# Experts' second layer with both weight halves in one 512-column product, and row transposes placed inside the first layer

## The reference, cut to what matters

```python
onehot = one_hot(argmax(softmax(t @ Wr)), 8)         # 4096 tokens, 8 experts
disp   = zeros(8 * 640, 256).at[flat].add(t * kept)  # 640 rows for each expert
h      = relu(einsum('ecd,edf->ecf', disp.reshape(8, 640, 256), W1))   # W1 256 x 1024
eout   = einsum('ecf,efd->ecd', h, W2)                                 # W2 1024 x 256
out    = where(kept, eout[flat] * pmax, t)
x      = layernorm(x + out)
```

## Time and profile before

| what | value |
|---|---|
| median of 3 runs | 936.65 us (935.19 to 936.7) |
| profiled execution, its own time | 935.7 us |
| span of its core | 933.9 us |
| mean granted TensorE clock | 0.937 |
| PE busy over the span | 791.7 us (85%) |
| experts' part of the span | 658 to 934 us |

### The profile page before, as it was taken

How to read it: one execution, slowest core, us unless ns; L and a number is a source line. 1 busy time by engine, 2 the same in 40 slices (tenths; PEclk the granted TensorE clock), 3 DMA queues, 4 the chain that set the end, 5 groups by cost and what they waited for, 6 DMA issues and landing times. The chain is left out here.

```text
span 933.9 us, 16891 instructions
## 1 busy us (share of the span) xinstructions
PE 791.7 (85%) x5933; PEld 632.4 (68%) x5933; DVE 581.5 (62%) x1410; ACT 402.1 (43%) x639; POOL 356.0 (38%) x290
## 2 busy tenths in 40 slices
PE   5999883589999999999999897872799999999992
PEld 3777662456666766666676664541699999999982
DVE  4888855465777777777777876532345554654542
ACT  4666540235545655555555555530433323422320
POOL 0333334433355545544545452232225134424422
PEclk9999887889999999999999999865799999999997
DMA  3115701554445434544554334003422243234000
GB/s 126 46 28 156 208 1 51 153 152 124 127 143 165 151 113 134 153 139 135 160 154 137 119 119 126 23 31 111 147 91 86 86 129 119 63 111 139 21 28 19
DMA packets 75913, 100.91 MB, mean 108 GB/s; under 512 B 10961, under 2 KB 63354, under 8 KB 75856
## 3 DMA queue, kind: packets, MB, share of 16 engines
q1 hardware_dynamic: 72400, 92.03, 33.1%
q0 software_dynamic: 3456, 8.13, 2.5%
HBM read 65.47 MB, written 35.74 MB: 108 GB/s over the span
## 5 line engine op out<-in xcount | busy, mean ns | idle before, releaser
L984 DVE TENSOR_REDUCE nmax<-ps_m 128x4 f32<-128x1024 f32 x128 | 156.6, 1223 | 52.5 <-PE ps_m L744 40.5
L938 ACT ACTIVATE pt<-ps_a 128x1024 f32<-128x1024 f32 x128 | 131.4, 1026 | 99.4 <-PE ps_a L754 75.8
L1249 ACT ACTIVATE hid<-ps_h 128x640 fp32r<-128x640 f32 x64 | 45.1, 705 | 151.0 <-PE ps_h L1189 151.0
L1189 PE MATMUL ps_h<-xt,w_hi 128*128 128x320 f32 x512 | 99.9, 317 | 1.0 <-DVE xt L1264 1.0
L1298 DVE SCALAR_TENSOR_TENSOR hid<-ps_h,hid 128x640 fp32r<-128x640 f32 x64 | 52.8, 824 | 56.0 <-ACT hid L1249 55.5
L744 PE MATMUL ps_m<-kst,qst 48*128 48x256 f32 x512 | 65.6, 334 | 25.6 <-DVE nmax L984 23.0
L1201 PE MATMUL ps_y<-w_hi,hid 128*128 128x256 f32 x640 | 85.3, 284 | 1.7 <-issue 1.7
L1189 PEld LDWEIGHTS ps_h<-xt,w_hi 128*128 128x128 f32 x512 | 79.9, 191 | 5.5 <-DVE hid L1298 3.0
L1201 PEld LDWEIGHTS ps_y<-w_hi,hid 128*128 128x128 f32 x640 | 80.1, 191 | 1.9 <-issue 1.9
L744 PEld LDWEIGHTS ps_m<-kst,qst 48*128 48x128 f32 x512 | 39.1, 188 | 61.3 <-DVE nmax L984 32.3
L621 POOL TENSOR_TENSOR half<-kq,half 128x512 fp32r<-128x512 f32 x32 | 41.6, 1301 | 96.6 <-ACT half L876 91.7
(11 more groups left out here) (169 smaller groups left out, 1586.9 us busy)
## 6 DMA issues: line engine op xcount, KB each, us to landing
halves_dram<-half SPq DMA_DIRECT2D x64, 256.0 KB, 2.5
gated<-in_w SPq DMA_DIRECT2D x16, 1024.0 KB, 5.4
kst<-halves_dram SPq DMA_DIRECT2D x64, 128.0 KB, 2.6
qst<-halves_dram SPq DMA_DIRECT2D x64, 128.0 KB, 3.0
rows_dram<-blank SPq DMA_DIRECT2D x1, 5160.0 KB, 19.6
gated<-rows_dram SPq DMA_DIRECT2D x8, 645.0 KB, 4.2
x_raw<-in_x_t SPq DMA_DIRECT2D x8, 512.0 KB, 3.9
xres<-in_x SPq DMA_DIRECT2D x16, 256.0 KB, 3.4
```

Source lines behind the costliest of these rows:

```text
L938: nc.scalar.activation(pt[:, k % 4].rearrange("p s t q -> p (s t q)"), ps_a[:].rearrange("p s t q -> p (s t q)"), ACT.Exp).then_inc(s["exp ...
L984: nc.vector.tensor_reduce(nmax[:, q, :, :, h // 2].rearrange("p t s -> p s t"), ps_m[:], AX.X, ALU.max, negate=True).then_inc(s["max_done" ...
L1189: mm = pe.matmul(ps_h[:, f % 2, c2, 0:HC], w1[a][:, p, k, f * P:(f + 1) * P], xt[:, b, p, k, c2 * HC:(c2 + 1) * HC], start=(n == 0 and k = ...
L1249: nc.scalar.activation(hid[:, HI, f, :].rearrange("p (c n) -> p c n", c=2), ps_h[:, f % 2, :, 0:HC], ACT.Relu).then_inc(s["hid_hi"], 1)
```

## The change

The two split halves of W2 become one tile in which, for each block f, the 256 high columns and the 256 low columns lie side by side. For each row tile `down` multiplies `hid` HI by all 512 columns (8 products; `hi*hi` into the first half of the bank, `hi*lo` into the second), then `hid` LO by the 256 high columns, added to the first half. For tile 0 the HI products wait block by block for `hid_hi`, and only the LO products wait for all of `hid_lo`. DVE adds the second half of the bank (times gate, plus row) into `res` first, raises `res_part`, waits for it, and adds the first half. The three turns of the next expert's rows now follow hidden blocks 4, 5 and 6 on PE, ACT and DVE alike; SP and POOL keep their order.

```diff
--- before.py
+++ after.py
@@ -1106,7 +1106,7 @@
     new = gated[:, 1, 0:2 * TS * D].rearrange("p (b t d) -> p b t d", b=2, t=TS)
     rows = gated[:, 3, 0:2 * TS * ROW].rearrange("p (b t r) -> p b t r", b=2, t=TS)
     w1 = [T("w1_hi", [P, 2, KD, F], F32R), T("w1_lo", [P, 2, KD, F], F32R)]
-    w2 = [T("w2_hi", [P, 2, FT, D], F32R), T("w2_lo", [P, 2, FT, D], F32R)]
+    w2 = T("w2", [P, 2, FT, 2, D], F32R)
     xt = T("xt3", [P, 2, 2, KD, CAP], F32R)
     hid = T("hid", [P, 2, FT, CAP], F32R)
     st, mv, ve = T("st4", [P, TS, 6], F32), T("mv4", [P, TS, 2], F32), T("ve4", [P, TS], F32)
@@ -1117,12 +1117,13 @@
     ps_h = PS("ps_h", [P, 2, 2, 512], F32)
     ps_y = PS("ps_y", [P, 2, 512], F32)
 
-    names = """rows_in0 rows_in1 turn_mm turn_hi turn_lo hid_mm hid_hi hid_lo w1_hi w1_lo w2_hi w2_lo out_mm res_done
+    names = """rows_in0 rows_in1 turn_mm turn_hi turn_lo hid_mm hid_hi hid_lo w1_hi w1_lo w2_hi w2_lo out_mm res_part res_done
         var_ready rstd new_done sent0 sent1 step3 token_done setup3 stats_done""".split()
     s = {n: sem("e_" + n) for n in names}
     rows_in, sent = ([s[n + str(i)] for i in range(2)] for n in ("rows_in", "sent"))
     w1_in, w2_in = c["w1_in"], c["w2_in"]
     TURNS = (TS + 1) // 2
+    TURN_AT = {FT - 1 - TURNS + i: i for i in range(TURNS)}
 
     def use(e, per, parity):
         if isinstance(e, int):
@@ -1167,17 +1168,17 @@
 
         @block.tensor
         def _(pe):
-            def turn_rows(e, p):
-                pe.wait_ge(rows_in[p], use(e, 16, p))
-                for i in range(TURNS):
-                    need(pe, s["turn_lo"], e * TURNS + i - 1)
-                    for t in range(2 * i, min(2 * i + 2, TS)):
-                        for k in range(KD):
-                            mm = pe.transpose(ps_t[:, (p * TURNS + i) % 2, (t % 2) * D + k * P:(t % 2) * D + (k + 1) * P],
-                                              rows[:, p, t, k * P:(k + 1) * P], eye[:])
-                    mm.then_inc(s["turn_mm"], 1)
-
-            def hidden(e, p):
+            def turn_rows(e, p, i):
+                if i == 0:
+                    pe.wait_ge(rows_in[p], use(e, 16, p))
+                need(pe, s["turn_lo"], e * TURNS + i - 1)
+                for t in range(2 * i, min(2 * i + 2, TS)):
+                    for k in range(KD):
+                        mm = pe.transpose(ps_t[:, (p * TURNS + i) % 2, (t % 2) * D + k * P:(t % 2) * D + (k + 1) * P],
+                                          rows[:, p, t, k * P:(k + 1) * P], eye[:])
+                mm.then_inc(s["turn_mm"], 1)
+
+            def hidden(e, p, last):
                 pe.wait_ge(s["w1_lo"], e + 1)
                 pe.wait_ge(s["turn_lo"], (e + 1) * TURNS)
                 for f in range(FT):
@@ -1190,24 +1191,31 @@
                                                xt[:, b, p, k, c2 * HC:(c2 + 1) * HC], start=(n == 0 and k == 0),
                                                stop=(n == 2 and k == KD - 1))
                     mm.then_inc(s["hid_mm"], 1)
+                    if f in TURN_AT and not last:
+                        turn_rows(e + 1, 1 - p, TURN_AT[f])
 
             def down(e, p):
                 pe.wait_ge(s["w2_lo"], e + 1)
-                pe.wait_ge(s["hid_lo"], (e + 1) * FT)
                 for t in range(TS):
                     need(pe, s["res_done"], e * TS + t - 1)
-                    for n, (a, b) in enumerate(PARTS):
-                        for f in range(FT):
-                            mm = pe.matmul(ps_y[:, (p + t) % 2, 0:D], hid[:, a, f, t * P:(t + 1) * P], w2[b][:, p, f, :],
-                                           start=(n == 0 and f == 0), stop=(n == 2 and f == FT - 1))
+                    for f in range(FT):
+                        if t == 0:
+                            pe.wait_ge(s["hid_hi"], e * FT + f + 1)
+                        pe.matmul(ps_y[:, (p + t) % 2, 0:2 * D], hid[:, HI, f, t * P:(t + 1) * P],
+                                  w2[:, p, f].rearrange("p a d -> p (a d)"), start=(f == 0), stop=False,
+                                  skip_group_check=True)
+                    if t == 0:
+                        pe.wait_ge(s["hid_lo"], (e + 1) * FT)
+                    for f in range(FT):
+                        mm = pe.matmul(ps_y[:, (p + t) % 2, 0:D], hid[:, LO, f, t * P:(t + 1) * P], w2[:, p, f, HI],
+                                       start=False, stop=(f == FT - 1), skip_group_check=True)
                     mm.then_inc(s["out_mm"], 1)
 
-            turn_rows(0, 0)
+            for i in range(TURNS):
+                turn_rows(0, 0, i)
 
             def step(e, p, last=False):
-                hidden(e, p)
-                if not last:
-                    turn_rows(e + 1, 1 - p)
+                hidden(e, p, last)
                 down(e, p)
 
             run(pe, step)
@@ -1221,12 +1229,11 @@
 
         @block.scalar
         def _(act):
-            def x_hi(e, p):
-                for i in range(TURNS):
-                    act.wait_ge(s["turn_mm"], e * TURNS + i + 1)
-                    need(act, s["hid_mm"], (e - 1) * FT)
-                    src, dst = turned(e, p, i)
-                    nc.scalar.copy(dst[HI], src).then_inc(s["turn_hi"], 1)
+            def x_hi(e, p, i):
+                act.wait_ge(s["turn_mm"], e * TURNS + i + 1)
+                need(act, s["hid_mm"], (e - 1) * FT)
+                src, dst = turned(e, p, i)
+                nc.scalar.copy(dst[HI], src).then_inc(s["turn_hi"], 1)
 
             def w1_hi(e, p):
                 act.wait_ge(w1_in, 16 * e + 16)
@@ -1236,10 +1243,11 @@
             def w2_hi(e, p):
                 act.wait_ge(w2_in, 16 * e + 16)
                 need(act, s["out_mm"], (e - 1) * TS)
-                nc.scalar.copy(flat(w2[HI][:, p]), flat(w2_raw)).then_inc(s["w2_hi"], 1)
+                nc.scalar.copy(w2[:, p, :, HI], w2_raw).then_inc(s["w2_hi"], 1)
 
             w1_hi(0, 0)
-            x_hi(0, 0)
+            for i in range(TURNS):
+                x_hi(0, 0, i)
             w2_hi(0, 0)
 
             def step(e, p, last=False):
@@ -1248,8 +1256,9 @@
                     need(act, s["out_mm"], e * TS)
                     nc.scalar.activation(hid[:, HI, f, :].rearrange("p (c n) -> p c n", c=2), ps_h[:, f % 2, :, 0:HC],
                                          ACT.Relu).then_inc(s["hid_hi"], 1)
+                    if f in TURN_AT and not last:
+                        x_hi(e + 1, 1 - p, TURN_AT[f])
                 if not last:
-                    x_hi(e + 1, 1 - p)
                     w1_hi(e + 1, 1 - p)
                     w2_hi(e + 1, 1 - p)
 
@@ -1257,11 +1266,10 @@
 
         @block.vector
         def _(dve):
-            def x_lo(e, p):
-                for i in range(TURNS):
-                    dve.wait_ge(s["turn_hi"], e * TURNS + i + 1)
-                    src, dst = turned(e, p, i)
-                    nc.vector.tensor_tensor(dst[LO], src, dst[HI].bitcast(F32), ALU.subtract).then_inc(s["turn_lo"], 1)
+            def x_lo(e, p, i):
+                dve.wait_ge(s["turn_hi"], e * TURNS + i + 1)
+                src, dst = turned(e, p, i)
+                nc.vector.tensor_tensor(dst[LO], src, dst[HI].bitcast(F32), ALU.subtract).then_inc(s["turn_lo"], 1)
 
             def w1_lo(e, p):
                 dve.wait_ge(s["w1_hi"], e + 1)
@@ -1289,7 +1297,8 @@
                     op.then_inc(s["new_done"], 1)
 
             w1_lo(0, 0)
-            x_lo(0, 0)
+            for i in range(TURNS):
+                x_lo(0, 0, i)
 
             def step(e, p, last=False):
                 before = not isinstance(e, int) or e > 0
@@ -1304,13 +1313,16 @@
                         mean_var(e - 1, 1 - p)
                     if 1 < f < 2 + TS and before:
                         norm(e - 1, 1 - p, f - 2)
-                if not last:
-                    x_lo(e + 1, 1 - p)
+                    if f in TURN_AT and not last:
+                        x_lo(e + 1, 1 - p, TURN_AT[f])
                 for t in range(TS):
 
                     dve.wait_ge(s["out_mm"], e * TS + t + 1)
+                    nc.vector.scalar_tensor_tensor(res[:, t, :], ps_y[:, (p + t) % 2, D:2 * D], rows[:, p, t, D + 1:D + 2],
+                                                   rows[:, p, t, 0:D], ALU.mult, ALU.add).then_inc(s["res_part"], 1)
+                    dve.wait_ge(s["res_part"], e * TS + t + 1)
                     nc.vector.scalar_tensor_tensor(res[:, t, :], ps_y[:, (p + t) % 2, 0:D], rows[:, p, t, D + 1:D + 2],
-                                                   rows[:, p, t, 0:D], ALU.mult, ALU.add).then_inc(s["res_done"], 1)
+                                                   res[:, t, :], ALU.mult, ALU.add).then_inc(s["res_done"], 1)
                     dve.wait_ge(s["res_done"], e * TS + t + 1)
                     op = nc.vector.bn_stats(st[:, t, :], res[:, t, :])
                     if t == TS - 1:
@@ -1330,7 +1342,7 @@
 
             def w2_lo(e, p):
```

(2 more changed lines are left out.)

## The result

The changed kernel takes **922.56 us** (median of 4 runs, 920.99 to 924.75) against 936.67 us of the kernel before beside it (935.19 to 938.51): a ratio of 0.9845, 95% interval 0.9821 to 0.9868. The forecast was 924.8, range 919 to 929.5. The profiled execution took 922.01 us, its span is 920.2 us, 13.7 less than before's 933.9.

A forecast was written before the change was run, and what follows sets the result against it. PE's work was taken to bound each expert. From the profiled 935.7 us: - 10.1 - 2.1 - 1.9 + 0.9 + 1.5 + 0.5 gave 924.5, or 925.4 from the runs' median; forecast 924.8 us, range 919 to 929.5.

The forecast's parts named there:

- The transposes: Between an expert's layers: turns behind blocks 4 to 6 save 1.68 us for each of experts 1 to 6, 10.1 us.
- the feared waits in the blocks: Hidden blocks or LO products wait on ACT or DVE: 929.8 or 934.9 us; chance of half hidden or worse 0.13.
- at 8.2 too: nothing is lost if no wait adds a tenth: Second layer: block 7's low part is ready at 8.2 us, just when the HI products end, so no loss.
- The last expert: Before its second layer: HI products fill the wait for block 7's relu and low part, 1.9 us gained.
- The second layer: Wide products cut a row tile from 2.88 to 2.83 us; 40 tiles give back 2.1 us.
- the pitch: Second layer: time per product, 0.233 us for 512 columns (from the mixer) and 0.120 for 256.
- The row load: Now needed after block 4: 0.5 us in hand, except in step 0, where PE idles and 0.9 us is lost.
- its rival: Rows late in every step, behind W2's load: 938.6 us, or 947.6 with clock falls; chance 0.06.
- The fall of the clock: Step 0: PE's idle time takes the clock to half over 3.4 us, 1.5 us lost (bounds 0 and 3.1).
- The second sum: DVE's extra sum, 40 x 0.48 us, lies beside PE; only the last tile's costs, 0.5 us at the end.
- slower: Whole kernel: the change makes it slower than before, chance 0.05.
- the rivals: Wide product near its columns (919.4 us, 0.11), transposes half hidden or worse (0.13), rows late in every step (0.06).

The follow-up runs named there:

- experiment 7: Changed kernel with expert 1's rows loaded ahead of its weights: 922.36 us; with tile 0's low products also waiting block by block: 920.57 us.
- Experiment 1: Changed kernel with one part only: transposes moved but second layer as before, 952.43 us; wide product but transposes behind block 7, 977.01 us.
- experiment 5: Kernel before rerun unaltered, 943.18 us; changed kernel rerun unaltered, 923.66 us; changed kernel with DVE's W1 low part behind tile 2, 932.14 us.
- experiment 4: Kernel before with DVE's sum of each row tile made twice, nothing else changed: 977.78 us, ratio 1.0328.

## Why the prediction was right, point by point

- **The transposes (10.1 us): right**, 10.1 measured, with the second layer at 15.58 us as worked out and none of the feared waits in the blocks. The margin "at 8.2 too: nothing is lost if no wait adds a tenth" was as thin as said: tile 0 of each expert is 0.08 us longer than the others, and not when its low products wait block by block (experiment 7). What the text did not say is that this gain needs the high products first. Experiment 1 shows that without them the same move loses.
- **The last expert (1.9): right**, 1.88.
- **The second layer (2.1): right in kind, too small.** 3.5 us measured. The term that was mis-sized is the pitch: 0.230 us instead of the mixer's 0.233, and 0.119 for the narrow ones behind them, so 2.79 us a tile where 2.83 was forecast, 0.04 less in each of 40 tiles. The Trainium skill's 0.216 (TensorE: Matmul & The Clock Gate, Back-to-back issue gap), which it gives for isolated products, does not agree with this trace: 0.230 is 17 ns beyond the columns. Nor does the 0.131 that it gives there for a stream of weight loads and products.
- **The row load (0.9 lost): right**, 1.0, and no other step waits for it. It nearly met its rival: W2's load was issued 0.3 us ahead of the next first layer (785.10 against 785.39) and not 1.0 (the store that DVE holds up, experiment 5, puts POOL's chain back). The rows behind it, issued at 789.9, still landed after 3.9 us.
- **The fall of the clock (1.5 lost): not in the first trace**, there in the second. The forecast had PE idle for 2.7 us in step 0; it was 1.7, because the clock had risen 5.7 us after the start of the first layer and not 3.7 as in the kernel before, and the blocks ended later. This step "I take the fall" and the pitch make up the difference: 11.2 forecast for the profiled execution, 13.7 measured; 1.5 for the clock, 1.4 for the second layer, less 0.4 for the later start of the experts, step 0 and the end.
- **The second sum (0.5 lost at the end, otherwise "beside PE"): right in its number and wrong in its reason.** The step counted DVE's busy time and asked when PE wants its bank. It did not ask what else DVE's delay would meet. (The "10 and 12 us free" of ACT and POOL are a misreading: in the earlier trace rows these are the us in which they are busy, and half of POOL's are this one instruction.) The 6.05 us of POOL's low part of W2, against 4.59 in step 0 of the same trace, were there to be read, and say that the two instructions kept each other out already. In the kernel before, 0.5 us more on DVE costs 40 us (experiment 4). It cost nothing here because the other half of the change moved DVE and POOL apart by 4 us. That it did was luck, as far as the forecast goes: "slower" had a mechanism that the rivals did not name.

## What to carry to other kernels

When the same instruction has two durations in one trace (4.6 and 6.1 us), find out what it overlaps with before moving anything on either engine: two instructions that exclude each other are a race for who is first, and here a few tenths decide over 3.4 us an expert in the wait alone and 5 to 6 when the clock falls with it, or 40 in the kernel. A wait that fixes the order is the cheapest cure. And judge the parts of a change together: here each alone was slower, because one was the cover, or the distance, that the other needed.

## What the runs showed of the hardware that was not expected

- VectorE's and GpSimd's `tensor_tensor` with both inputs in SBUF run one after the other: 2.27 and 4.63 us alone, 7.1 and 4.63 with GpSimd first, 2.27 and 6.05 to 6.6 with VectorE first. VectorE's record begins while it is still kept out; recorded starts 0.1 to 0.3 us ahead of GpSimd's are found with either outcome (796.11 against 796.40 lost, 687.01 against 687.14 won), 0.4 us ahead with one only.
- The same holds for GpSimd's indirect stores: 1.0 us alone, 2.4 to 3.0 us for each of the 44 that started while VectorE made W1's low part.
- The granted clock fell for 3.4 us after a wait of PE of 1.84 us in two experts of four, in each of the two kernels with only the transposes moved; not after any wait of 1.0 to 1.8 us (the holes of 1.4 us of the kernel before, 1.7 us in step 0 of the changed one), not after two waits of 2.0 us, and with 17 of 18 waits of 2.9 to 3.9 us, for 3.4 or 6.8 us. A fall of 3.4 us cost 1.5 us in row tiles of 256-column products and 1.7 in those with 512-column ones.
- A 512-column float32r product has a pitch of 0.230 us here and 0.233 in the mixer, at the same granted clock; the cause of the 3 ns was not looked for.
